# Weight splitting in the projection stage of a cross-attention and mixture-of-experts kernel: the places of four conversion steps on ScalarE and GpSimd

## The reference

```
y_dca, y_main = y[:, -16:], y[:, :-16]
kv_dca = y_dca @ Wkv_dca + bkv_dca            # 16 extra context tokens, weights of their own
q      = LN_head(x @ Wq + bq)                 # 16 heads of 32
k, v   = LN_head(y_main @ Wk + bk), y_main @ Wv + bv
ctx    = attn(q, k, v) + attn(q, LN_head(kv_dca.k), kv_dca.v)
out    = ctx @ Wo + bo
```

## Time and profile before

| what | us |
|---|---|
| median of 3 runs (lowest, highest) | 1087.1 (1086.47, 1091.04) |
| profiled execution, its own time | 1091.38 |
| its span, first to last instruction | 1089.7 |
| TensorE busy in the span | 937.6 (86%) |
| GpSimd, VectorE, ScalarE busy | 616.2, 647.4, 463.3 |
| mean granted TensorE clock | 0.947 of full speed |

### The profile page before, as it was taken

The page is one execution under the profiler, slowest core; times in us unless marked ns, Lnnn a source line. Parts: engine busy times, 40 slices in busy tenths (PEclk is TensorE's granted clock), DMA queues, the critical chain, the costliest instruction groups (busy, mean ns, idle before and its releaser), DMA issues. The chain is left out here.

```text
span 1089.7 us, 17150 instructions
## 1 busy us (share of the span) xinstructions
PE 937.6 (86%) x5077; PEld 403.4 (37%) x5078; DVE 647.4 (59%) x1025; ACT 463.3 (43%) x846; POOL 616.2 (57%) x566
## 2 busy tenths in 40 slices
PE   3788984898898898799984699999999999998498
PEld 1444441111121121266531245445445444553133
DVE  8777777787787884377652244444455554442078
ACT  2465565777777776333520022223223223223040
POOL 6465554466766764432064289898899993004700
PEclk9999995999999999899995899999999999999689
DMA  7135435344444321143345555555556553347703
GB/s 260 44 108 154 142 105 173 120 149 165 164 155 164 104 74 60 40 136 117 116 166 184 181 174 191 168 185 178 185 192 192 186 177 125 109 171 269 218 20 136
DMA packets 104521, 162.31 MB, mean 149 GB/s; under 512 B 10904, under 2 KB 53912, under 8 KB 104080
## 3 DMA queue, kind: packets, MB, share of 16 engines
q1 hardware_dynamic: 91520, 116.45, 32.7%
q0 software_dynamic: 12896, 45.10, 12.3%
q10 hardware_dynamic: 48, 0.05, 0.0%
HBM read 108.08 MB, written 53.48 MB: 148 GB/s over the span
## 5 line engine op out<-in xcount | busy, mean ns | idle before, releaser
L1048 DVE TENSOR_REDUCE nm<-a_psS 128x4 bf16<-128x1984 f32 x62 | 138.3, 2230 | 55.5 <-PE a_psS L1106 53.6
L1005 ACT ACTIVATE p_t<-a_psT 128x512 f32<-128x512 f32 x256 | 138.9, 595 | 67.5 <-PE a_psT L1121 65.8
L956 POOL TENSOR_TENSOR p_sum<-p_t,p_t 128x512 f32<-128x512 f32 x64 | 81.5, 1273 | 94.6 <-ACT p_t L1005 93.6
L1874 PE MATMUL e_psU<-w_exp,e_xT 128*128 x456 | 107.4, 386 | 7.7 <-issue 4.0
L1874 PE MATMUL e_psY<-w_exp,e_gT 128*128 x456 | 110.7, 379 | 0.9 <-ACT e_y L1815 0.9
L1874 PE MATMUL e_psG<-w_exp,e_uT 128*128 x456 | 104.9, 380 | 2.5 <-DVE e_uT L1829 2.5
L205 POOL TENSOR_TENSOR w_exp<-e_raw,w_exp 128x1024 f32 (+1 forms) x42 | 90.6, 2157 | 6.0 <-POOL e_raw L202 4.5
L1121 PE MATMUL a_psT<-q_stk,k_stk 98*128 98x512 f16 x256 | 85.6, 399 | 4.0 <-ACT p_t L1005 1.5
L197 POOL TENSOR_TENSOR w_exp<-e_raw,ws_tile 128x1024 f32 (+1 forms) x42 | 80.3, 1911 | 6.5 <-DMA e_raw<-in_L_ffn_Wup_dram 5.6
L1801 ACT ACTIVATE e_gT<-e_psGT 128x512 f16<-128x512 f32 x38 | 22.7, 597 | 123.4 <-PE e_psGT L1864 123.4
L1822 ACT ACTIVATE e_g<-e_g 128x512 f32<-128x512 f32 x38 | 23.9, 630 | 106.8 <-DVE e_g L1832 106.8
(11 more groups left out here) (326 smaller groups left out, 1816.0 us busy)
## 6 DMA issues: line engine op xcount, KB each, us to landing
xs_dram<-zero SPq DMA_DIRECT2D x38, 256.0 KB, 5.3
e_x<-xs_dram SPq DMA_DIRECT2D x38, 256.0 KB, 4.0
bias<-in_L_ffn_bup_dram SPq DMA_DIRECT2D x38, 256.0 KB, 3.8
bias<-in_L_ffn_bgate_dram SPq DMA_DIRECT2D x38, 256.0 KB, 3.7
ys_dram<-e_y SPq DMA_DIRECT2D x38, 256.0 KB, 3.8
q_dram<-q_st SPq DMA_DIRECT2D x24, 256.0 KB, 3.0
k_dram<-k_st SPq DMA_DIRECT2D x24, 256.0 KB, 3.7
q_stk<-q_dram SPq DMA_DIRECT2D x64, 96.0 KB
```

What stands on the lines that cost most here:

```text
L956: pool.tensor_tensor(p_sum[:, w % SUMS, :], probs(w, 0), probs(w, 1), ALU.add).then_inc(s["sum_1"], 1)
L1005: act.activation(probs(w, k), psT[:, k % 2], ACT.Exp, scale=SCALE / (QS * QS)).then_inc(s["exp"], 1)
L1048: dve.tensor_reduce(nm[:, i, :, 0:1].rearrange("p h o -> p (h o)"), psS[:, :, 0:NMAIN], AX.X, ALU.max, negate=True)
L1874: ins = pe.matmul(dst[:, :], stationary, moving, start=(k == 0 and chunks[0] == 0), stop=(k == len(terms) - 1 and chunks[-1] == KD - 1))
```

## The change

`dca_weights(j - 1)` moves from behind `mid(0, j - 1)` to the place in front of `mid(0, j)`, behind `back`, on ScalarE and on GpSimd. On both engines the steps for Wo leave the end of the first batch. ScalarE now makes them in the last batch, the high half in step j = 0 and the scaling in step j = 1, each in front of `mid`. GpSimd makes the low half in two instructions of 128x1024, in steps j = 2 and j = 3 of the last batch, in front of `mid`; its last batch leaves the hardware loop for that.

```diff
 (gpsimd)
+            def wo_low(half):
+                at = slice(half * KD // 2, (half + 1) * KD // 2)
+                pool.wait_ge(s["wo_16"], 1)
+                pool.tensor_tensor(wo[:, 1, at]..., wo_raw[:, at, :]..., wo[:, 0, at]..., ALU.subtract).then_inc(s["wo_lo"], 1)
-            def steps(b, first):
+            def steps(b, first, last):
                 for j in range(TB):
                     if not (first and j < 2):
                         back(*earlier(b, j, 2))
+                    if first and 0 < j <= KC:
+                        dca_weights(j - 1)
+                    if last and j >= TB - 2:
+                        wo_low(j - (TB - 2))
                     mid(b, j)
-                    if first and j < KC:
-                        dca_weights(j)
-            steps(0, True)
-            pool.wait_ge(s["wo_16"], 1)
-            pool.tensor_tensor(wo[:, 1]..., wo_raw..., wo[:, 0]..., ALU.subtract).then_inc(s["wo_lo"], 1)
-            with pool.Fori(1, B) as b:
-                steps(b, False)
+            steps(0, True, False)
+            with pool.Fori(1, B - 1) as b:
+                steps(b, False, False)
+            steps(B - 1, False, True)
 (scalar)
                         back(*earlier(b, j, 2))
+                    if first and 0 < j <= KC:
+                        dca_weights(j - 1)
+                    if last and j == 0:
+                        act.wait_ge(s["wo_ld"], 16)
+                        act.activation(wo[:, 0], wo_raw[:, :, :], ACT.Copy, scale=WS).then_inc(s["wo_hi"], 1)
+                    if last and j == 1:
+                        act.wait_ge(s["wo_hi"], 1)
+                        act.activation(wo_raw[:, :, :], wo_raw[:, :, :], ACT.Copy, scale=WS).then_inc(s["wo_16"], 1)
                     mid(b, j)
-                    if first and j < KC:
-                        dca_weights(j)
...
             steps(0, True, False)
-            act.wait_ge(s["wo_ld"], 16)
-            act.activation(wo[:, 0], wo_raw[:, :, :], ACT.Copy, scale=WS).then_inc(s["wo_hi"], 1)
-            act.wait_ge(s["wo_hi"], 1)
-            act.activation(wo_raw[:, :, :], wo_raw[:, :, :], ACT.Copy, scale=WS).then_inc(s["wo_16"], 1)
```

More of the change, by code:

```diff
@@ L468, in back @@
                                        buf[:, j // PAIR, 0, :, c:c + P], ALU.subtract).then_inc(s[dn], 1)
-            def steps(b, first):
+            def wo_low(half):
+                at = slice(half * KD // 2, (half + 1) * KD // 2)
+                pool.wait_ge(s["wo_16"], 1)
+                pool.tensor_tensor(wo[:, 1, at].rearrange("p k n -> p (k n)"), wo_raw[:, at, :].rearrange("p k n -> p (k n)"),
+                                   wo[:, 0, at].rearrange("p k n -> p (k n)"), ALU.subtract).then_inc(s["wo_lo"], 1)
+            def steps(b, first, last):
                 for j in range(TB):
@@ L473, in steps @@
                         back(*earlier(b, j, 2))
+                    if first and 0 < j <= KC:
+                        dca_weights(j - 1)
+                    if last and j >= TB - 2:
+                        wo_low(j - (TB - 2))
                     mid(b, j)
-                    if first and j < KC:
-                        dca_weights(j)
-            steps(0, True)
-            pool.wait_ge(s["wo_16"], 1)
-            pool.tensor_tensor(wo[:, 1].rearrange("p k n -> p (k n)"), wo_raw[:, :, :].rearrange("p k n -> p (k n)"),
-                               wo[:, 0].rearrange("p k n -> p (k n)"), ALU.subtract).then_inc(s["wo_lo"], 1)
-            with pool.Fori(1, B) as b:
-                steps(b, False)
+            steps(0, True, False)
+            with pool.Fori(1, B - 1) as b:
+                steps(b, False, False)
+            steps(B - 1, False, True)
             back(B - 1, TB - 2)
```

## The result

The changed kernel takes 1091.9 us (median of 20 runs, 1089.7 to 1093.9), the kernel before 1088.3 in the 20 runs beside it. The ratio is 1.0031, with a 95% interval of 1.0023 to 1.0039: 3.4 us slower by the ratio, 3.8 having been forecast, and less than the half per cent that I had called hard to tell from no change. With twenty runs of each it can be told. The forecast time was 1090.9, 1.0 under the measured one; the kernel before itself stands 1.2 higher here than in the three runs (1087.1) that the forecast was added to.

The account below looks back on a forecast made before the run. `project` was taken as bound by a chain of waits from one `hr` to the next, no engine being full. 5.1 lost less 1.3 gained made 3.8, added to the median 1087.1: 1090.9 us, range 1085.3 to 1095.3.

Parts of the forecast that it names:

- wdca steps, gain: First batch, tiles two and three: moving ScalarE's pairs gives 2.0, the second pair costs 2.15; gain taken as 0.1 us.
- Wo leaves batch one, gain: End of first batch: GpSimd's low half no longer stalls `xn`, shortening the `hr` interval 11.78 to 10.62; gain 1.16 us.
- Wo's copies on ScalarE, loss: Last batch, steps 0 and 1: copies delay squares by 1.92 each, 0.4 absorbed; loss 3.4 us, bounds 1.9 and 3.8.
- L687 blocked in step 2, loss: Last batch: VectorE's 128x32 scaling waits for GpSimd's first low half to end; worked out 1.0, summed as 0.9 us.
- L687 blocked in step 3, loss: Last batch: VectorE's 128x32 scaling waits for GpSimd's second low half, which starts later against the chain; estimated 1.5 us.
- last `hr` to barrier, gain: End of `project`: GpSimd, 5.8 us later, replaces SyncE as last at the barrier; 0.7 us of slack is used.
- `project`, loss: Whole stage before the barrier: 5.1 lost at its end less 1.3 gained in the first batch; 3.8 us slower.
- Rival 4: Wo's copies fit into waits after all and only batch one's gain stays: 1.3 us faster, 1085.8; chance 0.07.
- Rival 1: Last batch: VectorE's scaling L687 is not blocked by GpSimd's low halves: only 2.0 us slower, 1089.1; chance 0.22.
- rival 2: End of `project`: SyncE still sets the barrier, 1.9 late, less 1.3: 0.6 us slower, 1087.7; chance 0.08.
- Rival 3: New holes in TensorE's last-batch work lower its clock or delay its return: 7.6 us slower in all, 1094.7; chance 0.13.
- A criterion that was no good: Behind the barrier: the prediction was to count as wrong if those stages changed length by more than a microsecond.

Follow-up runs that it names:

- dca_only: Kernel before with only the wdca steps moved, Wo steps left in place; `project` 140.08 us against 140.15, ratio 0.9998.
- no_low: Changed kernel without Wo's low half on GpSimd (zeros in its place); `project` 141.23 us, ratio to the kernel before 1.0011.
- no_l687_end: Changed kernel with VectorE's scaling of hv taken over by ScalarE's root in the last two tiles; `project` 141.98 us, ratio to the kernel before 1.0037.
- low_in_waits: Changed kernel, ScalarE's Wo copies back behind batch one, low halves ahead of `back` in step 0 of batches three and four; `project` 138.79 us, ratio 1.0001.
- wdca_hidden: low_in_waits with both wdca chunks centred behind the first tile and ScalarE's second pair put into two waits; `project` 137.72 us, ratio 0.9985.
- copies_back: Changed kernel with ScalarE's two Wo copies back behind the first batch, low halves still in the last; `project` 139.99 us, ratio 0.9997.
- fold_only: Kernel before with the scaling of hv left to ScalarE's root in all 16 tiles, on another chip; `project` 138.92 us, ratio 1.0000.
- changed_again: Changed kernel unaltered, run again on another chip; 1052.49 us against 1049.05 for the kernel before, ratio 1.0029.
- no_l687_again: Repeat of no_l687_end on another chip, beside the changed kernel; 1051.48 us against 1049.05 for the kernel before, ratio 1.0026.

## Why the prediction was right, step by step

| step of the prediction | forecast | measured | from |
|---|---|---|---|
| wdca steps, gain | 0.1 | 0.1 | dca_only, `hr` one to four |
| Wo leaves batch one, gain | 1.16 | 1.17 | 11.78 to 10.61 |
| Wo's copies on ScalarE, loss | 3.4 | 3.18 | no_low, last four intervals |
| L687 blocked in step 2, loss | 0.9 | 0.89 | 1.07 - 0.18 |
| L687 blocked in step 3, loss | 1.5 | 1.46 | 1.64 - 0.18 |
| last `hr` to barrier, gain | 0.7 | 0.87 | 10.35 to 9.48 |
| `project`, loss | 3.8 | 3.38 | first `hr` to barrier |

**The waits.** The first pair and the copies were read rightly. That idle time stands ahead of only one of ScalarE's four new places was read rightly from the brackets of the earlier trace rows. GpSimd's waits existed too, and lay over VectorE's work. Rival 4, that all the copies fit into waits, falls with the two copies' 3.18.

**The block.** It was the step with the widest bounds (0.6 to 4.1), taken from the nearest form in the earlier trace rows. That L687 behaves like `xn` was an argument from a form sixteen times as large, and it held. The sizes came out within 0.04, which is closer than the working deserved: step 2 is worked out as 1.0 and stands in the sum as 0.9, and the 1.5 of step 3 was an estimate without a sum behind it. That the total agrees so well is in part luck. The block's size is shown by L696's two rows, its cause by three kernels: without the low half (no_low) the scaling is 0.18; with the low half and no scaling (no_l687_end) the chain runs on; with the low half moved (low_in_waits) neither costs anything. In wdca_hidden it appeared unplanned, where the same two forms meet. Over the 13 profiles the 128x32 scaling meets a running GpSimd instruction seven times and each time ends within 0.04 behind it; the other 165 take 0.18. Rival 1 falls with this. The rule that the prediction took from the Trainium skill (page SBUF — State Buffer, section Who interferes with whom), that such a tensor_scalar and GpSimd exclude each other for a whole instruction, agrees with these rows.

**The end.** The barrier falls at 178.01. GpSimd ends at 175.70 + 1.15 = 176.85, 1.16 before it, SyncE's stores long before, at 170.02 + 3.40 = 173.42, so rival 2 falls. Before, the barrier came 1.25 behind SyncE's end and 1.98 behind GpSimd's, as the prediction has it. SyncE's end moved less than forecast: from the first `hr` it is 138.90 before and 138.94 after, where 1.9 - 1.3 = 0.6 was expected; since SyncE no longer sets the end, this changed nothing. SyncE's last stores (compare):

```profile
170.02 3.40 SPq L323 DMA_DIRECT2D k_dram<-k_st  x3
```

**The two terms that were off.** The copies: I took 1.92 each, the pitch of one copy after another. What counts is the distance from a copy to the square behind it, 141.48 - 139.68 = 1.80, less than the copy's own 1.90, since the next activation starts before the last one's end. And the way from the last `hr` to the barrier shrank by 0.87, not 0.7: 0.73 is the slack between GpSimd and SyncE, 0.09 the shorter way from the last arrival to the barrier (1.16 instead of 1.25), and 0.05 lies between `hr` and GpSimd's end. Together they make the 0.4 between 3.8 and 3.38.

**Rival 3, the clock.** It did dip beside the first of the new holes in TensorE's work:

```profile
140.00:150.00 10.00, 8.90 (x42) 4.83 (x42) 6.48 (x15) 7.00 (x13) 4.51 (x5) 0.85 0.00 0
```

The 12 matmuls of `q` at 141.07 took 3.74. It cost nothing there: between 138 and 162 no instruction of VectorE waits for TensorE, so TensorE was ahead by more than it lost. Nor did it take the hole to make the dip. copies_back, which has no hole there, is granted 0.83 in the same stretch (the kernel before 1.00), and dca_only and fold_only, whose last batch has the order of the kernel before, take 3.37 and 3.85 for the same 12 matmuls; changed_again and no_l687_end have the hole and no dip beside it. The granted clock just behind the barrier is the same 0.50 in all profiles; how its return varies is in the last section.

**A criterion that was no good.** I wrote that the prediction is wrong if the stages behind the barrier change their length by over a microsecond. From the barrier to the end they take 916.4 before and 913.9 after; the kernel before itself takes 912.9 in its second profile. Over the ten profiles from chips where the kernel before takes 1088 to 1091 it is 911 to 918 whatever the kernel. The criterion measured the execution and not the change, and the sum was right in spite of it.

## What to carry to other kernels

Before work is moved "into an engine's wait", read the bracket ahead of the very instruction it is put before: an engine that is busy half of a stage may still come to that point with nothing idle, and then the work is paid in full. A GpSimd tensor operation also needs the other engine's view: put it where VectorE has no SBUF-only tensor_scalar on the chain (one of 128x32 was held for the whole rest of the GpSimd instruction, one of 128x1 was not), or take that operation off VectorE (here the root's own scale and bias did it for 0.09). A gain of one or two microseconds in a stage is to be measured in that stage, from a mark inside it, since the stages behind it move by more from one execution to the next.

## What the runs showed of the hardware that I had not expected

**The clock behind the barrier comes back at different times from execution to execution, and the next stage's length differs too.** TensorE mostly waits ahead of the barrier (busy for 2.14 of its last 10 us in the kernel before, for 2.60 in the changed one), and in all profiles the granted clock is 0.50, 1.2 GHz, in the first 20 us behind it. When it comes back to the higher level differs. The busy time by stretch of 5 us, before (barrier at 173.29) and no_l687_end (at 177.14), at the same distances from the barrier:

```profile
183.29:188.29 5.00, 4.15 (x15) 0.76 (x11) 3.77 (x3) 3.65 (x7) 1.72 (x2) 0.50 0.06 19
193.29:198.29 5.00, 5.00 (x30) 0.82 (x26) 3.49 (x3) 3.66 (x7) 1.51 (x2) 0.73 0.35 107
198.29:203.29 5.00, 3.43 (x28) 0.79 (x30) 2.32 (x3) 2.78 (x6) 1.16 (x2) 1.00 0.29 94
```

```profile
187.14:192.14 5.00, 4.15 (x15) 0.75 (x11) 3.78 (x3) 3.66 (x7) 1.72 (x2) 0.50 0.07 16
197.14:202.14 5.00, 5.00 (x24) 0.78 (x24) 2.72 (x3) 3.31 (x7) 1.16 (x2) 0.50 0.30 98
202.14:207.14 5.00, 3.43 (x28) 0.59 (x24) 2.00 (x2) 2.56 (x6) 1.09 (x1) 0.97 0.25 89
```

Ten microseconds behind the barrier the two are alike. In the stretch that begins 20 behind it one is granted 0.73 and has 30 matmuls, the other 0.50 and 24. Over the thirteen profiles that stretch has 0.50 to 0.73, and the way from the barrier to the first product with Wo is 279.75 to 283.55. Kernels with 0.50 there have 282.1 to 282.4 and, once, fold_only with 0.51, 283.55; those with 0.58 to 0.73 have 279.75 to 281.3. It does not order them all (the two with the highest clock there, 0.73, are at 281.3), so the clock explains a part at most, and what else does is open. Both profiles of no_l687_end are at 0.50 and both of the changed kernel above it (0.69 and 0.59). But the same kernel can do either: the kernel before has 0.73 and 281.29 in one profile, 0.50 and 282.28 in the other. So no edit is needed for such a difference; whether the edit had a part in it can't be said from two each.

**Another chip, another time.** changed_again, no_l687_again and fold_only ran on a chip where the kernel before takes 1049.05 instead of 1088 to 1091 on the others. The stretch from 520 to 1040 of changed_again has a granted clock of 0.98, where it is 0.94 in the changed kernel's first profile:

```profile
520.00:1040.00 520.00, 487.76 (x2434) 241.61 (x2433) 258.02 (x406) 155.77 (x268) 331.36 (x300) 0.98 0.55 182
```

The ratio of the changed kernel is the same on both, 1.0031 and 1.0029, so the comparison within one chip holds where the times themselves can't be compared.

**A tensor_scalar of 128x32 is large enough to be stopped, one of 128x1 was not.** The scaling of `ve`, one element per partition (L620 before the change), keeps its 0.15 beside the low half L479; with 32 elements the instruction took 1.07, 1.64 and 1.03. A reciprocal of 128x32 was not held either: in five cases beside a running low half it kept its 0.35. Where between 1 and 32 elements it changes was not tried.
